# Summing the squares of the queries inside ACT's squaring instruction instead of in a DVE reduction (attention and mixture-of-experts kernel, one core)

## The chip, the cores and the metric

The kernel runs on one core of one Trainium2 chip. The metric is the device time of one execution in microseconds (us), less is better. The engines are called by the profile's names: PE is TensorE, DVE is VectorE, ACT is ScalarE, POOL is GpSimd, SP is the engine that here only issues transfers.

## The reference

One layer of a transformer, in float32: cross attention with normalised queries and keys, then a mixture of 12 experts, of which each token takes two.

```python
def rms_norm(x, w, eps=1e-6):
    var = mean(x * x, axis=-1)
    return w * (x * rsqrt(var + eps))

# x: (64, 128, 512), ctx: (64, 128, 512); 16 query heads, 4 key/value heads, 128 wide
q = (layernorm(x) @ Wq)   # (64, 128, 16 heads, 128)
k, v = ctx @ Wk, ctx @ Wv # (64, 128, 4 heads, 128)
q, k = rms_norm(q, q_norm_w), rms_norm(k, k_norm_w)
probs = softmax(q @ k.T / sqrt(128))          # each key head serves 4 query heads
x = x + (probs @ v) @ Wo
x = x + experts(layernorm(x))                 # top 2 of 12, with a capacity for each
```

The change touches the sum over the 128 columns of each query head in `rms_norm`.

## The kernel before, in words

**Two stages.** The first stage, some 2300 us of the 2700, does the attention and the routing of one batch of 128 tokens after the other, 64 batches, with batches 3 to 61 in a hardware loop (`loop`, L580). The second stage (`experts`, L33) gathers the tokens of each expert, computes and scatters them. The change is in the first stage alone.

**The unit of work.** A batch has four units, g = 0 to 3, one for each key head with its four query heads. Every engine has a function `body(b)` that runs through g = 0 to 3 and lists, by hand, what this engine does in this unit, in this order. An engine takes its instructions strictly in that order; between engines there are semaphores. The lists work at different distances from the current unit: the scores, exponentials and probabilities are those of the unit itself, the output projection that of two units back (`last`), the widened probabilities and the product with v one back (`before`), the scaled queries two ahead (`near`), and the projection and squares of the queries three ahead (`far`).

**Precision.** Each operand of a matmul is split in a high part (a cast on ACT) and a low part (a subtraction on DVE or POOL), and three products are summed.

**The queries, step by step.** PE projects four heads of queries to a PSUM bank (`queries`, L744). ACT squares the bank into another, SQ_B (`square_q`, L868 to L874). DVE sums the squares of each head (`sum_q`, L1013 to L1017). POOL adds the epsilon (L1289) and raises to the power -1/2 (`rms_q`, L1283 to L1292). One unit later ACT scales the queries by it, head by head, to f16 (`split_q`, L876 to L883), DVE forms the low part (L1019 to L1026), and SP issues a transposing transfer of both parts (`turn_q`, L622).

**The probabilities, step by step.** PE computes the scores (L752). DVE takes the maximum of each row (L1032) and its negative (L1035). ACT does the exponentials, head by head, each with its row sum from the accumulator (`exps`, L885 to L893). DVE inverts the sums (L1041) and multiplies (L1044). ACT casts the result to f16 (`split_p`, L899), DVE subtracts for the low part (L1050), SP issues the transposing transfer (`turn_p`, L627 to L630), and in the next unit ACT and DVE widen the transposed tile (L905, L1057). PE multiplies it with v (L764), ACT and DVE split the outcome (`split_o`, L911 and L971), and PE does the output projection (L780).

**The lists around the change.** On ACT a unit is: split_o, widen_p, one of (split_xn2, split_v, split_k) where g is 0, 1 or 3, exps, `square_q` of three units ahead, split_x (x_hi, L850, g = 0) or split_c (c_hi, L845, g = 3), split_p, split_q, and square_k where g = 1. On DVE it is: maxima, split_o, widen_p, some steps once a batch, normalise, `sum_q` of three units ahead, split_p, split_q, and again some steps once a batch. On POOL: split_x (x_lo, L1266, g = 0) or split_c (c_lo, L1261, g = 3), then rms_q, then small steps.

**Semaphores at the change.** Before squaring, ACT waits until the sum of the unit before is done (q_ss), and in the unit whose squares are those of g = 1 also until DVE has summed the squares of the keys, which use the same bank. DVE waits for the squares (q_sqd) and until POOL has read the sums before (q_m).

Of the kernel before, what the change touches and what calls it, by code (L numbers as in the profile page):

```python
# [11 lines left out]
HPG = NH // NG  # L12
# [16 lines left out]
QS, KS, PS = 16.0, 64.0, 16384.0  # L29
# [370 lines left out]
def build(nc, x, xT, cT, wq, wk, wv, wo, qw, kw, gateT, w13, w2T, out):  # L400
    f32, f32r, bf16, f16, i32, u32 = (mybir.dt.float32, mybir.dt.float32r, mybir.dt.bfloat16,
                                      mybir.dt.float16, mybir.dt.int32, mybir.dt.uint32)
    ACT = mybir.ActivationFunctionType
    AX = mybir.AxisListType
# [5 lines left out]
    def wait(eng, sem, n, apart=False):  # L410

        if isinstance(n, int) and n <= 0:
            return
        if apart:
            wait_apart(eng, (sem, n))
        else:
            eng.wait_ge(sem, n)

    def wait_apart(eng, *pairs):


        with ExitStack() as regs:
            values = []
            for s, n in pairs:
                if not isinstance(n, int):
                    reg = regs.enter_context(eng.register(f"wait_{s.name}_{nc.next_id()}"))
                    eng.reg_add(reg, n, 0)
                    n = reg
                values.append((s, n))
            eng.wait_ge(s_const, 1)  # L430
            for s, n in values:
                if not (isinstance(n, int) and n <= 0):
                    eng.wait_ge(s, n)  # L433

    def live(b):
        return not isinstance(b, int) or 0 <= b < NB

    def off(b, g, k):

        return b + (g + k) // NG, (g + k) % NG  # L440

    keep = ExitStack()
    with keep:
        def sem(name):
            return keep.enter_context(nc.semaphore(name))
# [11 lines left out]
        with ExitStack() as ctx:  # L457
# [35 lines left out]
            def sm(n, dt=f32):  # L493
                v = small[:, at[0]:at[0] + n]
                at[0] += n
                return v if dt is f32 else v.bitcast(dt)

            smax, nmax, psums, rsums = sm(4), sm(4), sm(4), sm(4)
            q_ssq, q_ms, q_rms = sm(4), sm(4), [sm(4), sm(4)]
# [15 lines left out]
            Q_BS, K_B, V_B, S_B, OT_B, WO_B, SQ_B = pb[0:2], pb[2], pb[3], pb[4], pb[5], pb[6], pb[7]  # L515

            def heads(bank):
                return bank[:, :].rearrange("p (h t) -> p h t", h=HPG)
# [14 lines left out]
            k_sqd, k_ss, k_m, k_r, k_nrm, k_hi, k_lo = (sem(n) for n in (  # L533
                "k_squared", "k_sumsq", "k_meansq", "k_rms", "k_normed", "k_hi", "k_lo"))
            v_hi, v_lo = sem("v_hi"), sem("v_lo")
            q_sqd, q_ss, q_m, q_r, q_hi, q_lo = (sem(n) for n in (
                "q_squared", "q_sumsq", "q_meansq", "q_rms", "q_hi", "q_lo"))
            sc_done, mx_done, nm_done, exp_done, rs_done, p_nrm, p_hi, p_lo = (sem(n) for n in (
                "scores_done", "max_done", "negmax_done", "exp_done", "rsum_done", "probs_done", "p_hi", "p_lo"))
            pt_hi, pt_lo, ot_done, ot_hi, ot_lo = (sem(n) for n in ("pt_hi", "pt_lo", "ot_done", "ot_hi", "ot_lo"))  # L540
# [18 lines left out]
            def stage(l):  # L559
                flat = work[:, STAGES[l % NST], :]  # L560
                return flat if LOTS[l][0] == "o" else flat.rearrange("p (c n) -> p c n", c=NC)
# [277 lines left out]
            def _(act):  # L839
# [28 lines left out]
                def square_q(b, g):  # L868
                    u = 4 * b + g
                    wait(act, q_done, u + 1)  # L870
                    wait(act, q_ss, u)
                    if g == 1:
                        wait(act, k_ss, b + 1)
                    nc.scalar.activation(SQ_B[:, :], Q_BS[g % 2][:, :], ACT.Square, scale=1.0 / QS).then_inc(q_sqd, 1)  # L874

                def split_q(b, g):  # L876
                    u = 4 * b + g
# [90 lines left out]
            def _(dve):  # L968
# [33 lines left out]
                def split_k(b):  # L1002
                    wait(dve, k_hi, b + 1)
                    nc.vector.tensor_tensor(s16[:, LO, :], kn.rearrange("p (g t) -> p g t", g=NG), s16[:, HI, :],
                                            ALU.subtract).then_inc(k_lo, 1)

                def split_v(b):
                    wait(dve, v_hi, b + 1)
                    nc.vector.scalar_tensor_tensor(out=vp[1][:, :, :], in0=V_B[:, :].rearrange("p (g t) -> p g t", g=NG),
                                                   scalar=1.0 / PS, in1=vp[0][:, :, :].bitcast(f32),  # L1010
                                                   op0=ALU.mult, op1=ALU.subtract).then_inc(v_lo, 1)

                def sum_q(b, g):  # L1013
                    u = 4 * b + g
                    wait(dve, q_sqd, u + 1)
                    wait(dve, q_m, u)
                    nc.vector.tensor_reduce(q_ssq, heads(SQ_B), AX.X, ALU.add).then_inc(q_ss, 1)  # L1017

                def split_q(b, g):  # L1019
                    u = 4 * b + g  # L1020
# [7 lines left out]
                def maxima(b, g):  # L1028
                    u = 4 * b + g
                    wait(dve, sc_done, u + 1)  # L1030
                    wait(dve, nm_done, u)
                    nc.vector.tensor_reduce(smax, heads(S_B), AX.X, ALU.max).then_inc(mx_done, 1)  # L1032
                    wait(dve, mx_done, u + 1)
                    wait(dve, exp_done, u)
                    nc.vector.tensor_scalar(nmax, smax, esc, -1.0, ALU.mult, ALU.mult).then_inc(nm_done, 1)  # L1035
# [17 lines left out]
                def widen_p(b, g):  # L1053
                    u = 4 * b + g
                    wait(dve, d_pT, 16 * (u + 1))
                    wait(dve, ot_done, u)
                    nc.vector.tensor_copy(ptp[1][:, :, :], pT16[:, LO, :]).then_inc(pt_lo, 1)  # L1057

                def split_o(b, g):
                    wait(dve, ot_hi, 4 * b + g + 1)  # L1060
                    minus([p[:, :, :] for p in otp], heads(OT_B)).then_inc(ot_lo, 1)

                def residual(b):
                    wait(dve, wo_used, 4 * b + 4)
                    wait(dve, d_xr, 16 * (b + 1))
                    nc.vector.tensor_tensor(x_res, x_res, WO_B[:, :], ALU.add).then_inc(x1_done, 1)
# [9 lines left out]
                def norm2(b):  # L1076
                    wait(dve, r2_done, b + 1)
                    wait(dve, d_x1, 16 * (b + 1))
                    nc.vector.tensor_scalar(x_res, x_res, mv_2[:, 0:1], rstd_2, ALU.subtract,
                                            ALU.mult).then_inc(xn2_done, 1)  # L1080

                def split_xn2(b):
                    wait(dve, xh_done, b + 1)
                    nc.vector.tensor_tensor(s16[:, LO, :], x_res.rearrange(by_chunk, c=NC), s16[:, HI, :],
                                            ALU.subtract).then_inc(xl_done, 1)
# [89 lines left out]
                for l in range(NLOT):  # L1175
                    if l + 1 < NLOT and LOTS[l + 1][0] == "q":
                        n, part = LOTS[l + 1][1], stage(l + 1)
# [12 lines left out]

                def body(b):
                    for g in range(NG):
                        cur, near, far = (b, g), off(b, g, 2), off(b, g, 3)
                        before, last = off(b, g, -1), off(b, g, -2)
                        if g == 2 and live(b - 1):
                            residual(b - 1)
                        if live(b):
                            maxima(*cur)
                        if live(last[0]):
                            split_o(*last)  # L1200
                        if live(before[0]):
                            widen_p(*before)
                        if g == 0 and live(b - 2):
                            split_xn2(b - 2)
                        if g == 1 and live(b):
                            split_v(b)
                        if g == 3 and live(b + 1):
                            split_k(b + 1)
                        if g == 3 and live(b - 1):
                            norm2(b - 1)  # L1210
                        if live(b):
                            normalise(*cur)
                        if g == 2 and live(b - 2):
                            copy_logits(b - 2)
                        if g == 3 and live(b - 2):
                            count(b - 2)
                        if live(far[0]):
                            sum_q(*far)
                        if live(b):
                            split_p(*cur)  # L1220
                        if live(near[0]):
                            split_q(*near)
                        if g == 0 and live(b + 1):
                            stats_x(b + 1)
                        if g == 0 and live(b - 3):
                            place(b - 3)
                        if g == 1 and live(b + 1):
                            sum_k(b + 1)
                        if g == 2 and live(b + 1):
                            norm_k(b + 1)  # L1230
                        if g == 2 and live(b - 2):
                            choose(b - 2)
                        if g == 2 and live(b - 1):
                            stats_2(b - 1)

                loop(dve, body)


# [133 lines left out]
```

## Time and profile before

| what | value |
|---|---|
| median of 3 runs | 2702.43 us (2699.23 to 2703.63) |
| the profiled execution's own time | 2700.49 us |
| span of its trace | 2698.8 us |
| PE busy in the span | 2445.5 us (91%) |
| DVE busy | 2081.5 us (77%) |
| ACT busy | 1646.8 us (61%) |
| POOL busy | 1106.9 us (41%) |

The span is the time from the first to the last instruction of one profiled execution; the rest of its time lies around it. The granted clock of PE is at full speed through the first stage, after its start. Durations of instructions on one engine overlap at their ends, so the time that an instruction takes from its queue is read from the start of one to the start of the next. The name `pb` is any of the eight PSUM banks, `work` the tiles of SBUF that hold probabilities, f16 parts and raw inputs, and `small` the columns of statistics.

### The profile page before, as it was taken

The page shows a single profiled execution, that of the slowest core. Times are in us where ns is not written, and L with a number is a line of the kernel's source. Part 1 is how long each engine was busy: PE and PEld are TensorE (multiplying, and loading weights), DVE is VectorE, ACT ScalarE, POOL GpSimd, SP SyncE. Part 2 cuts the span into 40 slices and gives each one's busy share as a digit, 9 for nine tenths or more (in the row PEclk, how much of TensorE's full clock was granted, in tenths as well). Part 3 has the DMA queues.
Part 4 walks back from the last instruction along what each step waited for, and adds up shares of the span by engine and source line. Part 5 has one row for each costly group of instructions (what it writes and reads, how often), then busy time and mean ns, then how long its engine had stood idle before and what let it go on. Part 6 is the DMA issues. An engine that isn't in the chain of part 4 may idle for free. (4 is left out here: it accounts for less than half of the span.)

```text
span 2698.8 us, 51748 instructions
## 1 busy us (share of the span) xinstructions
PE 2445.5 (91%) x12985; PEld 1883.8 (70%) x12985; DVE 2081.5 (77%) x5478; ACT 1646.8 (61%) x4789; POOL 1106.9 (41%) x1279
## 2 busy tenths in 40 slices
PE   3899999999999999999999999999999999739983
PEld 3677777777777777777777777777777777525541
DVE  5678888888888888888888888888888888626652
ACT  4566666666666666666666666666666666515541
POOL 0334334333333443433333334344333333248885
PEclk8999999999999999999999999999999999968775
DMA  7455555555555555555555555555555555439997
GB/s 210 85 114 115 120 122 117 117 123 118 123 117 118 113 116 124 117 118 119 121 121 119 119 112 115 123 120 118 117 124 117 124 113 111 89 107 182 183 176 96
DMA packets 778098, 331.20 MB, mean 123 GB/s; under 512 B 695340, under 2 KB 707884, under 8 KB 778032
## 3 DMA queue, kind: packets, MB, share of 16 engines
q1 hardware_dynamic: 754960, 287.61, 47.9%
q0 software_dynamic: 22912, 43.16, 8.9%
q8 instruction: 13, 0.21, 0.0%
q14 instruction: 21, 0.17, 0.0%
q10 hardware_dynamic: 192, 0.04, 0.0%
HBM read 108.15 MB, written 57.71 MB: 61 GB/s over the span
## 5 line engine op out<-in xcount | busy, mean ns | idle before, releaser
L905 ACT CAST pt_hi<-work 128x512 fp32r<-128x512 f16 x256 | 159.0, 621 | 652.6 <-DMA work<-work 652.6
L891 ACT ACTIVATE work<-pb,small 128x128 f32<-128x128 f32 x1024 | 454.0, 454 | 47.2 <-DVE small L1035 47.0
L788 PE MATMUL pb<-wo_hi,ot_hi 128*128 128x512 f32 x1024 | 418.8, 409 | 34.9 <-DVE ot_lo L971 34.8
L716 PE MATMUL pb<-wq_hi,x_hi 128*128 128x512 f32 x1024 | 400.9, 391 | 29.7 <-POOL x_lo L1266 22.5
L788 PE MATMUL pb<-wo_hi,ot_lo 128*128 128x512 f32 x1024 | 400.7, 391 | 0.0
L788 PE MATMUL pb<-wo_lo,ot_hi 128*128 128x512 f32 x1024 | 400.4, 391 | 0.0
L716 PE MATMUL pb<-wq_lo,x_hi 128*128 128x512 f32 x1024 | 400.0, 391 | 0.0
L716 PE MATMUL pb<-wq_hi,x_lo 128*128 128x512 f32 x1024 | 399.6, 390 | 0.0
L1289 POOL TENSOR_TENSOR small<-small 128x4 f32<-128x4 f32 x256 | 170.7, 667 | 500.3 <-DVE small L1017 500.3
L1023 DVE SCALAR_TENSOR_TENSOR work<-pb,small,work 128x128 f16<-128x128 f32 x1024 | 286.9, 341 | 47.1 <-ACT work L881 47.1
L881 ACT ACTIVATE work<-pb,small 128x128 f16<-128x128 f32 x1024 | 290.5, 365 | 0.5 <-DMA work<-work 0.4
L1292 POOL TENSOR_TENSOR small<-small 128x4 f32<-128x4 f32 x256 | 258.4, 1009 | 29.5 <-POOL small L1289 18.7
L1050 DVE TENSOR_TENSOR work<-work 128x512 f16<-128x512 f32 x256 | 250.2, 977 | 17.6 <-ACT work L899 11.6
L788 PEld LDWEIGHTS pb<-wo_hi,ot_hi 128*128 128x128 f32 x1024 | 192.6, 188 | 95.6 <-DVE ot_lo L971 61.7
L1266 POOL TENSOR_TENSOR x_lo<-work,x_hi 128x512 fp32r<-128x512 f32 x64 | 82.6, 1291 | 425.9 <-ACT x_hi L850 379.5
L716 PEld LDWEIGHTS pb<-wq_hi,x_hi 128*128 128x128 f32 x1024 | 192.7, 188 | 80.4 <-issue 28.5
L760 PEld LDWEIGHTS pb<-work 128*128 128x128 f16 x3072 | 172.8, 98 | 99.9 <-issue 57.1
L760 PE MATMUL pb<-work 128*128 128x128 f16 x3072 | 216.5, 220 | 22.7 <-DMA work<-work 21.3
L716 PE MATMUL pb<-wkv_hi,c_hi 128*128 128x512 f32 x512 | 223.0, 435 | 0.0
L788 PEld LDWEIGHTS pb<-wo_hi,ot_lo 128*128 128x128 f32 x1024 | 192.9, 188 | 42.4
L716 PEld LDWEIGHTS pb<-wq_hi,x_lo 128*128 128x128 f32 x1024 | 192.8, 188 | 40.9
L716 PEld LDWEIGHTS pb<-wq_lo,x_hi 128*128 128x128 f32 x1024 | 192.8, 188 | 39.1
(144 smaller groups left out, 5307.0 us busy)
## 6 DMA issues: line engine op xcount, KB each, us to landing
work<-x SPq DMA_DIRECT2D x128, 256.0 KB, 3.4
work<-cT SPq DMA_DIRECT2D x64, 256.0 KB, 2.7
work<-xT SPq DMA_DIRECT2D x64, 256.0 KB, 3.1
out<-work SPq DMA_DIRECT2D x64, 256.0 KB, 4.1
xn_scratch<-work SPq DMA_DIRECT2D x64, 256.0 KB, 2.2
work<-work SPq DMA_TRANSPOSE x640, 3.0
work<-wq SPq DMA_DIRECT2D x16, 256.0 KB, 3.4
work<-wo SPq DMA_DIRECT2D x16, 256.0 KB, 3.6
```

What stands on the lines that cost most here:

```text
L716: mm = nc.tensor.matmul(bank[:, :], lhs[a][:, c, :], rhs[b_][:, c, :], start=(c == 0 and n == 0), stop=(c == NC - 1 and n == 2))
L760: mm = nc.tensor.matmul(S_B[:, h * 128:(h + 1) * 128], qT16[:, 4 * a + h, :], kT16[:, 4 * b_ + g, :], start=(n == 0), stop=(n == 2))
L788: mm = nc.tensor.matmul(WO_B[:, :], otp[a][:, h, :], wop[b_][:, g * HPG + h, :], start=(g == 0 and h == 0 and n == 0), stop=(g == NG - 1 a ...
L881: hi = nc.scalar.activation(q16[:, h, :], Q_BS[g % 2][:, h * 128:(h + 1) * 128], ACT.Copy, scale=q_rms[g % 2][:, h:h + 1])
L891: ex = nc.scalar.activation(probs[:, cols], S_B[:, cols], ACT.Exp, bias=nmax[:, h:h + 1], scale=esc, accum_out=psums[:, h:h + 1])
L905: nc.scalar.copy(ptp[0][:, :, :], pT16[:, HI, :]).then_inc(pt_hi, 1)
L1023: lo = nc.vector.scalar_tensor_tensor(out=q16[:, 4 + h, :], in0=Q_BS[g % 2][:, h * 128:(h + 1) * 128], scalar=q_rms[g % 2][:, h:h + 1], in ...
L1050: nc.vector.tensor_tensor(p16[:, LO, :], probs.rearrange("p (h t) -> p h t", h=HPG), p16[:, HI, :], ALU.subtract).then_inc(p_lo, 1)
L1266: nc.gpsimd.tensor_tensor(xp[1][:, :, :], raw_x.rearrange(by_chunk, c=NC), xp[0][:, :, :].bitcast(f32), ALU.subtract).then_inc(x_lo, 1)
L1289: nc.gpsimd.tensor_tensor(q_ms, q_ssq, eps_x.broadcast_to([128, HPG]), ALU.add).then_inc(q_m, 1)
L1292: nc.gpsimd.tensor_tensor(q_rms[g % 2], q_ms, neghalf, ALU.pow).then_inc(q_r, 1)
```

## The change

ACT squares each of the four heads in an instruction of its own, of 128 columns, and has the sum of the results written to that head's column of `q_ssq` by the accumulator output. The fourth raises q_ss. The sum on DVE is gone, with the semaphore q_sqd; ACT now waits itself until POOL has read the sums of the unit before (q_m).

```diff
-            q_sqd, q_ss, q_m, q_r, q_hi, q_lo = (sem(n) for n in (
-                "q_squared", "q_sumsq", "q_meansq", "q_rms", "q_hi", "q_lo"))
+            q_ss, q_m, q_r, q_hi, q_lo = (sem(n) for n in (
+                "q_sumsq", "q_meansq", "q_rms", "q_hi", "q_lo"))
...
                 def square_q(b, g):
                     u = 4 * b + g
                     wait(act, q_done, u + 1)
-                    wait(act, q_ss, u)
+                    wait(act, q_m, u)
                     if g == 1:
                         wait(act, k_ss, b + 1)
-                    nc.scalar.activation(SQ_B[:, :], Q_BS[g % 2][:, :], ACT.Square, scale=1.0 / QS).then_inc(q_sqd, 1)
+                    for h in range(HPG):
+                        cols = slice(h * 128, (h + 1) * 128)
+                        sq = nc.scalar.activation(SQ_B[:, cols], Q_BS[g % 2][:, cols], ACT.Square, scale=1.0 / QS,
+                                                  accum_out=q_ssq[:, h:h + 1])
+                    sq.then_inc(q_ss, 1)
...
-                def sum_q(b, g):
-                    u = 4 * b + g
-                    wait(dve, q_sqd, u + 1)
-                    wait(dve, q_m, u)
-                    nc.vector.tensor_reduce(q_ssq, heads(SQ_B), AX.X, ALU.add).then_inc(q_ss, 1)
-
...
-                        if live(far[0]):
-                            sum_q(*far)
                         if live(b):
                             split_p(*cur)
```

## Rows read from the trace of the kernel before

**Rows 1.** The windows view, 300 to 2100 us: busy us and instructions of each engine, granted clock

```profile
300.00:2100.00 1800.00, 1734.11 (x9649) 1369.51 (x9648) 1493.60 (x4171) 1190.51 (x3605) 697.71 (x865) 1.00 0.54 118
```

**Rows 2.** The waits view, 300 to 2100 us: total us, times, longest us

```profile
ACT pt_hi L905 <- DMA work<-work: 513.7, 203, 3.1
ACT work L899 <- DVE work L1044: 49.3, 102, 0.5
...
ACT ot_hi L911 <- PE pb L776: 2.1, 12, 0.2
...
DVE small L1041 <- ACT work L891: 154.4, 152, 1.4
...
DVE work L1050 <- ACT work L899: 8.2, 51, 0.2
...
PE pb L806 <- DVE ot_lo L971: 26.4, 51, 0.9
PE pb L788 <- DVE ot_lo L971: 24.2, 51, 0.5
PE pb L760 <- DMA work<-work: 15.2, 50, 0.3
```

**Rows 3.** The time line of ACT, units 3 and 0: start us, duration us, instruction

```profile
1351.89 0.46 ACT L891 ACTIVATE work<-pb,small 128x128 f32<-128x128 f32 x1 [0.64 <-DVE small L1035]
1352.25 0.19 ACT L891 ACTIVATION_READ_ACCUMULATOR work<-pb,small 128x1 f32 x1
1352.34 0.45 ACT L891 ACTIVATE work<-pb,small 128x128 f32<-128x128 f32 x1
...
1353.65 0.60 ACT L874 ACTIVATE pb<-pb 128x512 f32<-128x512 f32 x1
1354.16 0.62 ACT L845 CAST c_hi<-work 128x512 fp32r<-128x512 f32 x1
1354.73 0.62 ACT L899 CAST work<-work 128x512 f16<-128x512 f32 x1
...
1359.84 0.62 ACT L905 CAST pt_hi<-work 128x512 fp32r<-128x512 f16 x1 [2.88 <-DMA work<-work]
...
1362.64 0.60 ACT L874 ACTIVATE pb<-pb 128x512 f32<-128x512 f32 x1
1363.15 0.62 ACT L850 CAST x_hi<-work 128x512 fp32r<-128x512 f32 x1
1363.80 0.62 ACT L899 CAST work<-work 128x512 f16<-128x512 f32 x1
```

**Rows 4.** The time line of DVE: L1050 in units 2, 3, 0, the sum in unit 3

```profile
1346.06 0.69 DVE L1050 TENSOR_TENSOR work<-work 128x512 f16<-128x512 f32 x1
...
1354.79 0.68 DVE L1017 TENSOR_REDUCE small<-pb 128x4 f32<-128x512 f32 x1
1355.39 1.30 DVE L1050 TENSOR_TENSOR work<-work 128x512 f16<-128x512 f32 x1
...
1364.45 1.23 DVE L1050 TENSOR_TENSOR work<-work 128x512 f16<-128x512 f32 x1 [0.16 <-ACT work L899]
```

**Rows 5.** Groups of instructions by line, ACT: count, busy us, mean ns, idle before them

```profile
L891 ACT ACTIVATE work<-pb,small 128x128 f32<-128x128 f32 x1024 | 454.0, 454 | 47.2 <-DVE small L1035 47.0
L881 ACT ACTIVATE work<-pb,small 128x128 f16<-128x128 f32 x1024 | 290.5, 365 | 0.5 <-DMA work<-work 0.4
L891 ACT ACTIVATION_READ_ACCUMULATOR work<-pb,small 128x1 f32 x1024 | 205.2, 200 | 0.0
```

**Rows 6.** The time line of ACT, unit 2: the square and the cast of the probabilities

```profile
1344.33 0.60 ACT L874 ACTIVATE pb<-pb 128x512 f32<-128x512 f32 x1
1345.41 0.62 ACT L899 CAST work<-work 128x512 f16<-128x512 f32 x1 [0.48 <-DVE work L1044]
```

**Rows 7.** The time line of POOL, units 3 and 0: the subtractions for c_lo and x_lo

```profile
1354.86 1.29 POOL L1261 TENSOR_TENSOR c_lo<-work,c_hi 128x512 fp32r<-128x512 f32 x1 [2.73 <-ACT c_hi L845]
...
1363.85 1.29 POOL L1266 TENSOR_TENSOR x_lo<-work,x_hi 128x512 fp32r<-128x512 f32 x1 [6.00 <-ACT x_hi L850]
```

More of the change, by code:

```diff
@@ L1192, in body @@
                     for g in range(NG):
-                        cur, near, far = (b, g), off(b, g, 2), off(b, g, 3)
+                        cur, near = (b, g), off(b, g, 2)
                         before, last = off(b, g, -1), off(b, g, -2)
```

## The prediction

> **What bounds the kernel now.** The window view of the middle 1800 us comes first [rows 1]. PE is busy 1734 us of them (96%), DVE 1494 us (83%), ACT 1191 us (66%), POOL 39%. By shares alone the edit looks good: it takes work from the fuller of the two vector engines and gives it to the emptier one. Shares are averages, so the waits of the same window come next [rows 2]. The reader is to see who waits for whom. PE waits only for DVE's ot_lo and for a transposed tile, 66 us in all. ACT and DVE almost never wait for PE: ACT has 2.1 us of it, DVE has none. So PE hangs on the others and they do not hang on it. Between themselves they form a ring: ACT waits 513.7 us, 203 times, for the transposed probabilities (pT), DVE waits 154.4 us for ACT's exponentials (L1041), ACT waits 49.3 us for DVE's normalised probabilities (L1044, before L899), and DVE waits 8.2 us for ACT's cast L899.
>
> The ring runs once per unit (one group of four heads, four units to a batch), by the program's order: pT lands; ACT widens it (L905) and, behind that in its queue, does the exponentials; DVE normalises; ACT casts (L899); DVE subtracts (L1050); SP issues the transpose; pT lands, about 3.15 us after the subtraction ends (1356.69 to 1359.84) [rows 3, 4]. Nothing in it is a matmul. A batch takes 1800/51 = 35.3 us (51 waits of the once-per-batch kind [rows 2]), so what is added to the ring per batch is added to the time some sixty times. The time lines show where in the ring the edit falls. I count units 0 to 3 by the g of the body.
>
> **The change, part by part.** *Removed: one DVE sum (L1017) per unit.* It starts at 1354.79 in unit 3 and the next DVE instruction, L1050, at 1355.39: 0.60 us of DVE's queue, 256 times, 154 us in all [rows 4]. It stands between the normalisation and the subtraction L1050. But L1050 needs ACT's cast L899, which in unit 3 runs 1354.73 + 0.62 = 1355.35 [rows 3], 0.04 us before L1050 starts. The sum fills time in which DVE would wait for that cast anyway. In unit 0 DVE even waits 0.16 us more after it. I take the gain as zero; its cover is the cast, and if the cast were not there it would be 0.60 us per unit. The semaphore between square and sum goes too; POOL's first step then follows ACT. POOL gets its sums earlier, but the scales are used a unit later and no ACT wait on them is in the list of waits, so this is zero too.
>
> *Added: ACT's one square of 512 columns becomes four of 128, each with a read of the accumulator.* The square occupies 1354.16 - 1353.65 = 0.51 us of the queue now [rows 3]. The trace has no square with a sum, so its price is bounded. The nearest row is the exponential L891: 454 ns, 128 columns, two operands from `small`, an accumulator read behind it [rows 5]. The read starts 0.36 us after the exponential and the next exponential 0.09 us after the read [rows 3]; one occupies (1353.65 - 1351.89)/4 = 0.44 us. The scaling copy L881 has one operand from `small` and lasts 365 ns, 89 less than the exponential. The square has none, so I take another 89 off: 276 ns. Less the overlap of 0.10 (0.454 against 0.36) and plus 0.09 for the read that is 0.27 us each, 1.08 for four. Lowest: the read hides wholly, 0.18 each, 0.72 for four. Upper for my own case: the second 89 ns is not saved, 0.36 each, 1.44. The highest end, a whole exponential, 0.44 each, 1.76, is a rival. I take 0.27, as the operand step is read from two rows. So ACT's queue gets 1.08 - 0.51 = **0.57 us longer per unit**.
>
> *Where it lies.* Units 1 and 2: ACT idles 0.48 us before L899, waiting for L1044 [rows 2, 6]. From the start of the square to the start of L899 are 1345.41 - 1344.33 = 1.08 us. The four squares just fit: zero, and 4p - 1.08 if one takes p and p is above 0.27.
>
> Unit 3: after the square comes the cast of the next context, c_hi (L845, starts 1354.16), then L899 at 1354.73. There is 0.05 us of slack at most. c_hi starts 0.57 later. POOL's subtraction c_lo (L1261) starts at 1354.86, within 0.1 us of c_hi's end, and runs 1.29 us to 1356.15 [rows 7]. It matters, because L1050 lasts 1.30 us here, against 0.69 in unit 2, and ends at 1356.69, 0.54 us after POOL: it seems to stand still until POOL is through [rows 4, 6, 7]. So its end moves with c_hi: +0.57. Behind it the transpose is issued 0.57 later, pT lands 0.57 later, and unit 0's L905 and exponentials start 0.57 later.
>
> Unit 0 repeats this: square at 1362.64, x_hi (L850) at 1363.15 [rows 3], POOL's x_lo (L1266) 1363.85 to 1365.14 [rows 7], L1050 ending at 1364.45 + 1.23 = 1365.68, again 0.54 us after POOL. Another +0.57.
>
> One rule of the pages bears on this. The Trainium skill, "SBUF — State Buffer", section "Who interferes with whom", says that a DVE instruction with two SBUF inputs and a GpSimd instruction that reads SBUF exclude each other, and that the one that starts first holds the other off for its whole length. By that rule the trace agrees (end of L1050 = end of POOL + 0.54, twice). Had L1050 only been slower in itself, the shift would go through L899 alone, which has 0.09 us of slack in unit 3 (0.05 in ACT's queue, 0.04 in DVE's) and 0.13 in unit 0 (it starts at 1363.80, and could at 1363.67): some 0.92 us per batch and 56 us in all instead of 70.
>
> *Order and queues.* The new wait of the square (POOL's first step of the unit before) is met a unit earlier, as POOL works in order and is idle most of a unit: zero. The wait that keeps the key squares from the shared bank is now met by ACT's own earlier instruction. Behind the longer square stand, in ACT's queue, c_hi or x_hi, L899, the scaling copies and ot_hi. Those last feed PE through DVE's ot_lo, and PE will wait longer there, as a result and not as a cause. SP's queue is only moved with L1050; no transfer is added or changes place.
>
> **The sum.** 0.57 + 0.57 + 0 + 0 = 1.14 us per batch. c_hi is cast in unit 3 of 62 batches, x_hi in unit 0 of 63; the first one or two run behind the loading of weights. I take 61: 61 x 1.14 = **70 us**. The profiled execution took 2700.49 us (span 2698.8, 1.7 around it), which gives 2770; the median of the runs shown is 1.9 us higher, 2702.43, so 2772. Bounds of my case: at 0.18 each, 0.21 x 2 = 0.42 per batch, 26 us, 2728; at 0.36 each, (0.93 + 0.36) x 2 = 2.58 per batch, 157 us, 2860.
>
> **The rivals.** *Faster, by DVE's queue.* Place: L1050 in unit 3, where DVE has no idle time at all and L1050 starts the instant the sum ends. If DVE's own order sets that moment, 0.60 us fall away in that unit: 61 x 0.60 = 37 us, 2666. For it: 83% busy, and L1041 does not wait there (152 waits for 203 units [rows 2]). Against it: the cast ends 0.04 us before, and POOL's pass holds L1050 beyond that. It would decide only if the four squares took no more of ACT than the one (0.13 us each) and POOL did not hold L1050. The Trainium skill, "Perfetto Trace Analysis", section "Optimizing Scalar/DVE Operations", says that if DVE is saturated, moving work to Scalar may make sense; no row shows DVE saturated where this work lies, since it waits in three units of four.
>
> *No change.* ACT waits 513.7/51 = 10.1 us per batch for pT, and PE is 96% busy. If either were true slack, 1.14 us would vanish in it: 2702. Against it: the landing of pT is itself released by L1050, so it moves with ACT; and PE waits for DVE.
>
> *A whole exponential's price.* At 0.44 each: 1.76 - 0.51 = 1.25 twice, and 1.76 - 1.08 = 0.68 twice, 3.86 per batch, 235 us, 2938. For it: it is the one measured form with a sum. Against: the operand step of 89 ns.
>
> That the change does not do what it says I set aside; the sums and the order are plain in the diff.
>
> **How the numbers follow.** My case 0.80, faster 0.06, no change 0.07, the full exponential 0.07. The three rivals are the 0.20 that may be left out, so the range is my case's own, 2728 to 2860. A measurement of this kernel can tell about 0.2% from no change. Slower: 0.80 + 0.07 = 0.87; same 0.07; faster 0.06.
>
> **What would show it.** Right: square rows of about 276 ns with reads of 0.20; the ACT queue from the first square to c_hi about 1.08 us; L1050 in units 3 and 0 still ending 0.54 us after POOL, and now waiting for L899 in all units; ACT's idle time before L899 near zero; PE's waits for ot_lo up by about 1 us per batch with PE's busy share down to 93%; a batch of 36.4 us. Wrong: a batch still at 35.3 us, ACT's wait for pT shorter by what the squares cost, or L1050 in unit 3 earlier against L1041 than now.

## The result and the profile after

The change made the kernel slower: 2791.7 us (median of 4 runs, 2789.7 to 2793.0) against 2701.3 us, ratio 1.033 (95% interval 1.032 to 1.035), 90 us more. The forecast was 2772 us with a range from 2728 to 2860.

The windows view of the kernel after, 300 to 2100 us, with the same columns as [rows 1]:

```profile
300.00:2100.00 1800.00, 1678.12 (x9261) 1312.47 (x9260) 1327.05 (x3794) 1238.91 (x4822) 612.21 (x829) 1.00 0.52 114
```

PE is busy 93% of the time and not 96%, at the same granted clock. DVE went from 83% to 74%, ACT only from 66% to 69%. DVE got its relief, and it bought nothing. The waits of the same window are to be read beside [rows 2]; the line numbers have shifted, so that ACT's widening cast is L909, the cast of the probabilities L903, and DVE's subtraction L1048:

```profile
ACT pt_hi L909 <- DMA work<-work: 524.0, 195, 3.3
...
DVE work L1048 <- ACT work L903: 179.7, 195, 1.3
DVE small L1039 <- ACT work L895: 158.3, 147, 1.6
...
PE pb L716 <- DVE work L1021: 44.2, 49, 0.9
PE pb L806 <- DVE ot_lo L975: 37.3, 48, 1.2
PE pb L788 <- DVE ot_lo L975: 25.0, 49, 0.5
PE pb L760 <- DMA work<-work: 15.3, 50, 0.3
```

The reader is to see two things. DVE's wait for ACT's cast rose from 8.2 us to 179.7 us, about 0.92 us per unit: the time of the removed sum (0.60 us) and, in units 3 and 0, that of the longer squares stand there as idle time. And ACT no longer waits for DVE's L1044 at all (49.3 us before): its idle time before the cast is used up. The groups of ACT instructions, as in [rows 5], have the new work:

```profile
L876 ACT ACTIVATE pb<-pb 128x128 f32<-128x128 f32 x1024 | 283.2, 277 | 18.4 <-PE pb L716 18.4
...
L876 ACT ACTIVATION_READ_ACCUMULATOR pb<-pb 128x1 f32 x1024 | 201.8, 197 | 0.0
```

Next the time line of ACT in unit 3, as in [rows 3] (of the four squares the first two stand here), and the instructions of POOL and DVE behind it, as in [rows 7] and [rows 4]:

```profile
1369.57 0.28 ACT L876 ACTIVATE pb<-pb 128x128 f32<-128x128 f32 x1
1369.76 0.20 ACT L876 ACTIVATION_READ_ACCUMULATOR pb<-pb 128x1 f32 x1
1369.85 0.28 ACT L876 ACTIVATE pb<-pb 128x128 f32<-128x128 f32 x1
...
1370.70 0.62 ACT L845 CAST c_hi<-work 128x512 fp32r<-128x512 f32 x1
1371.21 0.63 ACT L903 CAST work<-work 128x512 f16<-128x512 f32 x1
...
1376.38 0.62 ACT L909 CAST pt_hi<-work 128x512 fp32r<-128x512 f16 x1 [2.94 <-DMA work<-work]
```

```profile
1371.39 1.28 POOL L1257 TENSOR_TENSOR c_lo<-work,c_hi 128x512 fp32r<-128x512 f32 x1 [3.35 <-ACT c_hi L845]
```

```profile
1371.87 1.35 DVE L1048 TENSOR_TENSOR work<-work 128x512 f16<-128x512 f32 x1 [1.08 <-ACT work L903]
```

The squares take 1370.70 - 1369.57 = 1.13 us of ACT's queue, where the one square took 0.51. POOL's pass ends at 1372.67 and L1048 at 1373.22, again 0.55 us later, though DVE had stood idle 1.08 us before it.

**Where the 90 us are.** The table is worked out from the traces: for each unit between 300 and 2100 us, the time from the start of the widening cast pt_hi to the start of the next one (one turn of the ring), split at the end of DVE's subtraction (L1050 of before); means over about 50 batches, in us.

| unit | before: to the end of the subtraction + to pT | after | more |
|---|---|---|---|
| 0 | 5.84 + 3.27 = 9.11 | 6.45 + 3.28 = 9.73 | 0.62 |
| 1 | 5.19 + 3.30 = 8.49 | 5.23 + 3.51 = 8.74 | 0.25 |
| 2 | 4.73 + 3.27 = 8.00 | 4.75 + 3.28 = 8.03 | 0.03 |
| 3 | 6.70 + 3.15 = 9.85 | 7.29 + 3.15 = 10.44 | 0.60 |
| batch | 35.45 | 36.94 | 1.49 |

61 x 1.49 = 91 us, the whole of the result. (From the first pt_hi to the last, the trace after is 93.2 us longer than the one before, and all that lies behind the last is 1.9 us shorter.) Units 0 and 3 are as argued. In unit 1, 0.21 of the 0.25 us lie behind the subtraction, in the transposing transfer. Nothing of that was forecast.

### The profile page after: what moved, and what is told of

It is laid out like the page before. It is cut to its first block and busy times, and to the rows that moved or that the text cites. A ratio compares the mean times of both kernels' runs of the same rounds, so it can differ in the third digit from the quotient of the medians.

```text
span 2790.4 us, 53029 instructions
## 1 busy us (share of the span) xinstructions
PE 2462.0 (88%) x12985; PEld 1877.6 (67%) x12985; DVE 1943.4 (70%) x5222; ACT 1773.9 (64%) x6581; POOL 1029.9 (37%) x1279
## 5 line engine op out<-in xcount | busy, mean ns | idle before, releaser
L909 ACT CAST pt_hi<-work 128x512 fp32r<-128x512 f16 x256 | 159.0, 621 | 686.9 <-DMA work<-work 686.9
L716 PE MATMUL pb<-wq_hi,x_hi 128*128 128x512 f32 x1024 | 409.3, 400 | 85.0 <-DVE work L1021 63.0
L1048 DVE TENSOR_TENSOR work<-work 128x512 f16<-128x512 f32 x256 | 259.9, 1015 | 237.5 <-ACT work L903 237.5
L716 PE MATMUL pb<-wq_hi,x_lo 128*128 128x512 f32 x1024 | 400.8, 391 | 0.0
L716 PE MATMUL pb<-wq_lo,x_hi 128*128 128x512 f32 x1024 | 400.8, 391 | 0.0
L1021 DVE SCALAR_TENSOR_TENSOR work<-pb,small,work 128x128 f16<-128x128 f32 x1024 | 286.8, 341 | 53.6 <-ACT work L885 53.6
L1285 POOL TENSOR_TENSOR small<-small 128x4 f32<-128x4 f32 x256 | 107.3, 419 | 524.8 <-ACT pb L876 524.8
L716 PEld LDWEIGHTS pb<-wq_hi,x_hi 128*128 128x128 f32 x1024 | 193.4, 189 | 155.5 <-DVE work L1021 84.0
L876 ACT ACTIVATE pb<-pb 128x128 f32<-128x128 f32 x1024 | 283.2, 277 | 18.4 <-PE pb L716 18.4
L1288 POOL TENSOR_TENSOR small<-small 128x4 f32<-128x4 f32 x256 | 258.0, 1008 | 29.5 <-POOL small L1285 18.7
L716 PE MATMUL pb<-wkv_hi,c_hi 128*128 128x512 f32 x512 | 223.3, 436 | 0.1
L716 PEld LDWEIGHTS pb<-wq_hi,x_lo 128*128 128x128 f32 x1024 | 193.4, 189 | 41.7
```

Source lines behind the costliest of these rows:

```text
L716: mm = nc.tensor.matmul(bank[:, :], lhs[a][:, c, :], rhs[b_][:, c, :], start=(c == 0 and n == 0), stop=(c == NC - 1 and n == 2))
L876: sq = nc.scalar.activation(SQ_B[:, cols], Q_BS[g % 2][:, cols], ACT.Square, scale=1.0 / QS, accum_out=q_ssq[:, h:h + 1])
L909: nc.scalar.copy(ptp[0][:, :, :], pT16[:, HI, :]).then_inc(pt_hi, 1)
L1021: lo = nc.vector.scalar_tensor_tensor(out=q16[:, 4 + h, :], in0=Q_BS[g % 2][:, h * 128:(h + 1) * 128], scalar=q_rms[g % 2][:, h:h + 1], in ...
L1048: nc.vector.tensor_tensor(p16[:, LO, :], probs.rearrange("p (h t) -> p h t", h=HPG), p16[:, HI, :], ALU.subtract).then_inc(p_lo, 1)
L1285: nc.gpsimd.tensor_tensor(q_ms, q_ssq, eps_x.broadcast_to([128, HPG]), ALU.add).then_inc(q_m, 1)
```

## The experiments

Each run was compared with the kernel before on the same chip; its median there was between 2690 and 2700 us, so ratios are what is compared, not times. Where an edit speaks of "the kernel after", it starts from the changed kernel.

### The removed sum by itself: sum_gone

On the kernel after, ACT squares all 512 columns in one instruction again, and no engine sums; the norms of the queries are left out.

```diff
+                nc.vector.memset(q_ssq, 1.0)
...
-                    for h in range(HPG):
...
-                    sq.then_inc(q_ss, 1)
+                    nc.scalar.activation(SQ_B[:, :], Q_BS[g % 2][:, :], ACT.Square, scale=1.0 / QS).then_inc(q_ss, 1)
```

> The kernel after, with ACT's square again one instruction of 512 columns and no sum of the squares on any engine (the sums are left at a constant, so the norms of the queries are left out). It shows the removal of DVE's sum alone. My theory, that ACT's cast covers the sum: 2701 us as before, or up to 13 us more if POOL's scatter, which now comes earlier, lengthens the transpose of unit 1. Rival, that DVE's own queue set L1050 in unit 3: 61 x 0.60 = 37 us less, 2664.

Measured: ratio 1.019 (1.017 to 1.021), 52 us slower than before. The scatter had been allowed at most 13 us. Less work on DVE, the square on ACT as it was, and slower. Three units are as before (9.13, 7.99, 9.83 us), and so is unit 1 up to the end of the subtraction (5.19); but there the transpose took 4.18 us from issue to landing, where it takes 3.23 in before and 3.44 in the kernel after. SP's and POOL's time lines show what changed: the issue of the transpose, and the start of the scatter. First of before, then of the kernel after, then of this run:

```profile
1374.28 1.24 SPq L630 DMA_TRANSPOSE work<-work  x1
```

```profile
1375.61 1.11 POOL L1304 DMA_INDIRECT token_table<-small  x1 [0.18 <-issue]
```

```profile
1354.52 1.24 SPq L630 DMA_TRANSPOSE work<-work  x1
```

```profile
1354.85 1.11 POOL L1300 DMA_INDIRECT token_table<-small  x1 [0.19 <-issue]
```

```profile
1371.52 1.25 SPq L630 DMA_TRANSPOSE work<-work  x1
```

```profile
1371.48 1.11 POOL L1297 DMA_INDIRECT token_table<-small  x1 [0.19 <-issue]
```

Once a batch, in unit 1, POOL scatters routing entries, behind rms_q in its queue. rms_q waits for the sum of the squares. In before the scatter starts 1.33 us after the issue of the transpose; in the kernel after the sums come from ACT earlier and it starts 0.33 us after; here 0.04 us ahead. This offset hardly varies over the trace (for the kernel after from 0.32 to 0.33 us).

### The same without the collision: sum_gone_scatter_late and scatter_late

```diff
+                        if g == 1 and live(b + 1):
+                            rms_k(b + 1)
                         if g == 1 and live(b - 3):
                             scatter(b - 3)
-                        if g == 1 and live(b + 1):
-                            rms_k(b + 1)
```

> The kernel without any sum of the squares, in which the scatter started 0.04 us before the issue of the transpose and that transpose took 4.18 us, with the scatters moved behind rms_k in the same way. Theory of the collision: the transpose takes 3.2 us again, a batch 35.4 us, the time that of before (ratio 1.000, within 0.3%). That would leave nothing for the removed sum itself. If the sum had been worth 0.60 us in unit 3, it would show now: ratio 0.986. If the scatter is not the cause: ratio 1.019 as before.

Measured: 0.9986 (0.9976 to 0.9996). The scatter starts 3.63 us after the issue, the transpose takes 3.23 us, a batch 35.43 us. So the sum on DVE, removed at no cost elsewhere, is worth 0.14%, and no more than 0.24% by the interval: it was covered, as forecast. The same move of the scatters on the kernel after:

> The kernel after, with POOL's two scatters moved behind rms_k in unit 1, so that they start some 4 us after the transpose of the probabilities is issued and not 0.3 us. Theory of the collision: issue to landing in unit 1 goes from 3.44 back to 3.2 us, 0.21 x 61 = 13 us less than the kernel after (ratio 1.033 of before becomes 1.028). If the longer transpose came from something else, the loads say: no change, 1.033.

Measured: 1.029 (1.028 to 1.031); unit 1 went from 8.74 to 8.53 us, the transpose from 3.44 to 3.23. The collision is thus 0.21 x 61 = 13 us of the 90 by the traces (by the two ratios 10 us, give or take 6), and the rest, some 77 us, is the length of the squares.

### What the length of the squares costs: four_squares and both_sums

```diff
-                    nc.scalar.activation(SQ_B[:, :], Q_BS[g % 2][:, :], ACT.Square, scale=1.0 / QS).then_inc(q_sqd, 1)
+                    for h in range(HPG):
+                        cols = slice(h * 128, (h + 1) * 128)
+                        sq = nc.scalar.activation(SQ_B[:, cols], Q_BS[g % 2][:, cols], ACT.Square, scale=1.0 / QS)
+                    sq.then_inc(q_sqd, 1)
```

> The kernel before, with the square cut in four of 128 columns without accumulator, and DVE's sum kept. In the kernel after one square with its read took 0.28 us of the queue, of which the read about 0.09; so 0.19 each, 0.76 for four, 0.25 more than the one. In units 3 and 0 that is 0.50 per batch, 61 x 0.50 = 30 us: 2731. If only the accumulator reads cost anything: 2701.

Measured: 1.009 (1.007 to 1.011), 24 us; a batch 0.34 us longer, nearly all of it in units 3 and 0. The time line of ACT in unit 3:

```profile
1367.77 0.78 ACT L876 ACTIVATE pb<-pb 128x128 f32<-128x128 f32 x4
1368.43 0.65 ACT L845 CAST c_hi<-work 128x512 fp32r<-128x512 f32 x1
```

The four take 0.66 us, 0.165 each and not 0.19. Cutting the square costs 0.15 us a unit, and the accumulator reads the rest of the 0.62: 1.13 - 0.66 = 0.47, or 0.12 each. I had put a read at 0.09.

both_sums is this edit with the accumulator output and the wait for q_m added, and DVE's sum kept.

> The accumulating squares on ACT and DVE's sum as well. My theory: DVE's sum is hidden behind the later cast, and the ring is longer by ACT alone. As POOL starts again only after DVE's sum, its scatter should not move against the transpose in unit 1: 2779 us, with 3.2 us from issue to landing there. If the scatter has nothing to do with it: 2792. If DVE's sum had been a saving in the kernel after: 2792 + 37 = 2829.

Measured: 1.032 (1.030 to 1.033), 2776 us against 2691 on that chip. Unit 0 took 9.75 us, unit 3 10.35, as in the kernel after (9.73, 10.44). The transpose of unit 1 took 3.22 us with POOL again behind DVE's sum (offset 1.34 us), which is the collision theory's mark. But units 1 and 2 (8.62 and 8.12 us) were each 0.09 us longer than with the scatter late: DVE's sum can start only when the longer squares are through, and so it ends after ACT's cast, which no longer covers all of it. In unit 3, 0.06 us of this come back. The collision that is missing and the sum that is no longer hidden nearly cancel, and the time alone, which I had set as the test, would not have told them apart; the transfer's time does.

### Place and not load: hybrid

In the bodies g = 1 and 2 (queries of g = 0 and 1) accumulating squares, in the others the square and the sum of before:

```diff
+                    if g >= 2:
+                        nc.scalar.activation(SQ_B[:, :], Q_BS[g % 2][:, :], ACT.Square,
+                                             scale=1.0 / QS).then_inc(q_sqd, 1)
+                        return
+                    wait(act, q_m, u)
+                    for h in range(HPG):
...
-                        if live(far[0]):
+                        if live(far[0]) and far[1] >= 2:
                             sum_q(*far)
```

> The accumulating squares only in the bodies g = 1 and g = 2, where ACT idled 0.48 us; in g = 3 and g = 0 the square and DVE's sum stay as before. My theory: 0.06 us per batch, 4 us, and 13 more if the earlier scatter of unit 1 lengthens the transpose: 2705 to 2718. Rival, that it is ACT's load as such and not the place: half of what the change cost, 2746.

Measured: 1.008 (1.006 to 1.010), 22 us, a quarter of the change for half of its instructions. This is just above the forecast (ratio 1.006 at most). Of 0.37 us per batch 0.21 are the collision (3.43 us in unit 1, offset 0.33), 0.06 the squares, and 0.08 are in unit 3. These last stand in front of the exponentials and not at the squares. DVE's maximum starts 0.2 us after the instruction ahead of it and not 0.1, as the same two rows show, first of before, then of this run, and ACT waits for it:

```profile
1350.80 0.18 DVE L1074 BATCH_NORM_AGGREGATE small<-small 128x2 f32<-128x6 f32 x1
1350.90 0.69 DVE L1032 TENSOR_REDUCE small<-pb 128x4 f32<-128x512 f32 x1
```

```profile
1364.55 0.18 DVE L1083 BATCH_NORM_AGGREGATE small<-small 128x2 f32<-128x6 f32 x1
1364.76 0.69 DVE L1041 TENSOR_REDUCE small<-pb 128x4 f32<-128x512 f32 x1
```

```profile
1365.75 0.46 ACT L900 ACTIVATE work<-pb,small 128x128 f32<-128x128 f32 x1 [0.82 <-DVE small L1044]
```

What DVE does in the extra 0.1 us is not shown. The same 0.62 us of ACT cost about 0.6 in units 0 and 3 of the kernel after and 0.02 to 0.04 in units 1 and 2, in both kernels.

### What holds DVE's subtraction: the casts first

```diff
-                        if live(far[0]):
-                            square_q(*far)
                         if g == 0 and live(b + 1):
                             split_x(b + 1)
                         if g == 3 and live(b + 2):
                             split_c(b + 2)
+                        if live(far[0]):
+                            square_q(*far)
```

On the kernel after:

> The kernel after, with the same two casts ahead of the four squares. By my theory the casts, and POOL behind them, are early again, L899 is late by the squares, and L1050 then starts after POOL is through and takes 0.69 us: it ends 1.64 + 0.62 + 0.03 + 0.69 = 2.98 us after the exponentials, against 3.04 in the kernel before. So units 3 and 0 cost what they cost before, and what is left is 0.06 of the squares and 0.21 of the collision in units 1 and 2: some 10 us over before, ratio 1.004, against 1.033 of the change. If L1050 were slow in itself (1.3 us in these units whatever POOL does): 1.2 us per batch more, ratio 1.031.

Measured: 1.0065 (1.004 to 1.009) against 1.033: one change of order gives back most of the loss. Unit 0 is 9.05 us and unit 3 9.79, both 0.06 below before, as worked out. DVE in unit 3 and in unit 0, and POOL's passes beside it:

```profile
1364.14 0.69 DVE L1048 TENSOR_TENSOR work<-work 128x512 f16<-128x512 f32 x1
1373.06 0.69 DVE L1048 TENSOR_TENSOR work<-work 128x512 f16<-128x512 f32 x1 [1.25 <-ACT work L903]
```

```profile
1362.55 1.50 POOL L1257 TENSOR_TENSOR c_lo<-work,c_hi 128x512 fp32r<-128x512 f32 x1 [2.23 <-ACT c_hi L845]
1371.46 1.50 POOL L1262 TENSOR_TENSOR x_lo<-work,x_hi 128x512 fp32r<-128x512 f32 x1 [5.76 <-ACT x_hi L850]
```

The subtraction takes 0.69 us in these units too, once POOL is through before it starts (at 1364.05 and 1372.96). Its 1.3 us were a wait. Unit 1 took 8.87 us, 0.13 more than in the kernel after, of which I had not thought. The traces show where: with unit 0 shorter, DVE comes late to the maximum of unit 1. L1033 starts 0.89 us after pt_hi instead of 0.46, and the exponentials 1.16 us after it instead of 1.01 (means of 50 batches). So part of what unit 0 gains meets DVE's own queue one unit later.

On the kernel before:

> The kernel before, with c_hi and x_hi cast ahead of the square on ACT in units 3 and 0. My theory, that POOL's subtraction behind these casts holds L1050: POOL's pass starts 0.51 us earlier in both units, L1050 ends 1.98 + 0.54 = 2.52 us after the exponentials leave ACT's queue and not 3.04; 1.04 us per batch, 63 us less (ratio 0.977), if PE, which then waits for less than 1 us per batch, doesn't take over; with that 0.977 to 0.985. If L1050 is just slow in these units or follows the cast L899 alone: no change, ratio 1.000.

Measured: 1.0023 (1.001 to 1.003). A miss: not 63 us less but 6 more. Unit 0 gained 0.29 us and not 0.52, unit 3 lost 0.37. DVE in unit 3, and POOL in units 3 and 0:

```profile
1356.65 0.69 DVE L1044 SCALAR_TENSOR_TENSOR work<-work,small 128x512 f32<-128x512 f32 x1
1357.26 0.17 DVE L1113 TENSOR_TENSOR small<-pb,small 128x24 f32<-128x24 f32 x1
1357.35 1.17 DVE L1115 TENSOR_TENSOR macc<-macc,small 128x24 bf16<-128x24 bf16 x1
1358.44 0.68 DVE L1017 TENSOR_REDUCE small<-pb 128x4 f32<-128x512 f32 x1
1359.04 0.68 DVE L1050 TENSOR_TENSOR work<-work 128x512 f16<-128x512 f32 x1
```

```profile
1356.98 1.50 POOL L1261 TENSOR_TENSOR c_lo<-work,c_hi 128x512 fp32r<-128x512 f32 x1 [2.22 <-ACT c_hi L845]
...
1366.37 1.50 POOL L1266 TENSOR_TENSOR x_lo<-work,x_hi 128x512 fp32r<-128x512 f32 x1 [5.50 <-ACT x_hi L850]
```

POOL's pass, begun while L1044 ran, takes 1.50 and not 1.29 us, in both units; in unit 0 that is what is missing of the gain. And in unit 3 a tiny instruction, L1115, 160 ns in the mean before, stands 1.17 us, until POOL ends at 1358.48. L1113 just ahead of it, with one input from PSUM, runs through in 0.17. The sum L1017 and L1050 stand behind L1115. Here, for once, DVE's sum is on the ring.

### Untangling it: x_first, c_before_exps, count_behind

x_first moves split_x alone, and leaves unit 3 as in before.

> The kernel before, with x_hi alone cast ahead of the square, in unit 0; unit 3 as before. In the run with both casts first, unit 0 fell from 9.11 to 8.82 us and unit 3 rose from 9.85 to 10.22, because POOL's earlier pass there held DVE's update of the expert counts (L1115), with the sum L1017 behind it. My theory: unit 0 keeps its 0.29 us and unit 3 is 9.85 again: 61 x 0.29 = 18 us less, ratio 0.993. If the two units are not independent: 1.000.

Measured: 0.9930 (0.991 to 0.995), 19 us less; unit 0 8.84 us, unit 3 9.81.

c_before_exps adds to it:

```diff
+                        if g == 3 and live(b + 2):
+                            split_c(b + 2)
                         if live(b):
                             exps(*cur)
```

> The kernel before, with x_hi ahead of the square in unit 0 and c_hi ahead of the exponentials in unit 3, where ACT idles 0.64 us for DVE. POOL's pass for c_lo then runs beside DVE's L1004 and not beside L1050. My theory: L1004 is held 0.3 us, L1050 takes 0.69 instead of 1.30 us and ends 0.28 us earlier; with the 0.29 of unit 0 0.57 per batch, 35 us less, ratio 0.987. If PE takes over, which waited 1.3 us per batch: between that and 0.993.

Measured: 0.9982 (0.997 to 0.999), a miss, and worse than x_first: unit 0 as there, unit 3 10.03 us. L1050 did take 0.69 us. But POOL, early now, caught another instruction of DVE, the cast L1057:

```profile
1350.87 1.29 DVE L1057 CAST pt_lo<-work 128x512 fp32r<-128x512 f16 x1
```

```profile
1350.59 1.29 POOL L1261 TENSOR_TENSOR c_lo<-work,c_hi 128x512 fp32r<-128x512 f32 x1
```

The cast takes 0.42 us elsewhere and 1.29 here, and this delay of 0.87 us is on DVE's path to L1044. I had only reckoned with instructions that read SBUF twice. The Trainium skill, "SBUF — State Buffer", section "Who interferes with whom", lists casts among the instructions that can enter a mode in which DVE takes the ports that it shares with GpSimd. By that the trace agrees (0.42 us against 1.29), and read against every DVE instruction in reach of POOL's pass it could have warned of the miss.

after_best is this order on the kernel after, with the scatters late.

> The kernel after with the same order of the casts and the scatters behind rms_k. Unit 3: the normalised probabilities are there 1.35 us after the exponentials leave ACT's queue, the four squares take 1.13 of it, so they are hidden, and L1050 ends 0.3 us earlier than in before. Unit 0: as in the run of the kernel after with the casts first, 0.06 less than before. Units 1 and 2: 0.07 more. Sum -0.3 per batch, 18 us less than before, ratio 0.993; so with this order too, the kernel with DVE's sum is the faster of the two. If the accumulating form were better once nothing waits for it: below 0.987.

Measured: 1.0063 (1.005 to 1.008), also a miss by the same mechanism (the same cast held for 1.29 us; unit 3 9.99 us). The comparison with c_before_exps holds: with the same casts in the same places the accumulating form is 0.8% behind the form with DVE's sum, though its scatters are out of the way.

count_behind has both casts first and takes the held instruction out of the way:

```diff
-                        if g == 3 and live(b - 2):
-                            count(b - 2)
                         if live(far[0]):
                             sum_q(*far)
                         if live(b):
                             split_p(*cur)
+                        if g == 3 and live(b - 2):
+                            count(b - 2)
```

> The kernel before, with both casts ahead of the square, and with DVE's update of the expert counts (L1113, L1115) moved behind the subtraction L1050 in unit 3. With the casts alone moved, POOL's pass for c_lo began between DVE's L1044 and L1115, held L1115 for 1 us, and the sum and L1050 stood behind it. My theory: with the counts out of the way L1050 is what POOL holds, it ends about 2.74 us after the exponentials leave ACT's queue as in unit 0, and not 3.04; unit 3 is 9.55 us, unit 0 8.82, together 0.59 per batch, 36 us less than before, ratio 0.987. If the cause of the slower unit 3 was another: ratio 1.002 as with the casts alone.

Measured: 0.9876 (0.986 to 0.989), 2665 us against 2700 on its chip, 35 us less: the fastest version of this study, with DVE's sum in it. DVE and POOL in unit 3:

```profile
1371.49 0.69 DVE L1017 TENSOR_REDUCE small<-pb 128x4 f32<-128x512 f32 x1
1372.09 0.99 DVE L1050 TENSOR_TENSOR work<-work 128x512 f16<-128x512 f32 x1
```

```profile
1371.04 1.50 POOL L1261 TENSOR_TENSOR c_lo<-work,c_hi 128x512 fp32r<-128x512 f32 x1 [2.22 <-ACT c_hi L845]
```

L1050 is held again, until 0.54 us after POOL's end (1372.54 and 1373.08), but earlier than in before. The split is not quite as foretold: unit 3 is 9.69 us, not 9.55, and unit 2 is 0.12 shorter by its transfer; the total of 0.55 per batch agrees with the 0.59 expected. The two belong together. In unit 3 the exponentials wait for DVE's maximum and not for the transfer, here as in before ([rows 3], the 0.64 us), so a tile that lands 0.13 us earlier only waits: the exponentials start 2.03 us after pt_hi, where they start 1.87 after it with the casts alone moved. PE now waits 50.5 us in the window for the moved counts. That costs nothing that can be seen, as unit 0 (8.84 us) and unit 1 (8.50 us) are as long as without it; but PE has hardly another wait left and is 97% busy, so little more can be won in the ring.

## Why the prediction was right, point by point

**The bound.** PE hangs on a ring of ACT, DVE, POOL and one transfer. Right: a batch took 35.45 us before and 36.94 after, the difference stands unit by unit in the ring, and PE merely waited more. One arc of it was misread: in unit 3 the exponentials hang on DVE's queue and its maximum (L1035), and not on the landing of pT, as the row with 0.64 us in [rows 3] already shows. It cost the forecast nothing, since nothing in unit 2 was moved, but count_behind and after_casts_first met it.

**The removed sum is covered.** Right, by sum_gone_scatter_late: 0.14%, at most 0.24%, where DVE's own queue would have given 1.4%. This also settles the rival that forecast a faster kernel. The cover holds in this order only: in before_casts_first the sum stood on the ring.

**The semaphore and POOL's order: zero.** This step failed. I saw that POOL gets its sums earlier and asked only who uses the scales. The question left out was what stands behind rms_q in POOL's queue: the scatter, which came 1 us earlier and met the transpose of unit 1. It cost 13 us here, and 52 us in sum_gone, where it came 0.37 us earlier still. The prediction also said that SP's queue only moves with L1050, which was true; the two transfers meet from different queues.

**The price of the squares.** The estimate of 276 ns for one was right (277). Its place in the queue was 0.28 us and not 0.27, because the read takes 0.12 and not 0.09 of it (four_squares). Four are 1.13 us, 0.62 more than the one; 0.57 was forecast. In units 0 and 3 that is 0.05 each, 6 us of the sum. In units 1 and 2, 1.13 no longer fits in the 1.08 us there: measured 0.04 + 0.02, some 3 us.

**The sum.** 70 forecast; 70 + 6 + 3 + 13 = 92, against 90 measured. That the scatter fell inside the range is luck: the range was made from the price of a square alone. The rivals "no change" and "a whole exponential's price" (0.44 each) fell with the measured 0.28.

**Who holds L1050.** Right, and the larger part of what there was to learn. L1050 ended 0.54 to 0.55 us after POOL in before, in the kernel after and in count_behind, and took 0.69 us where POOL was through. But I weighed this wait on one instruction only. POOL's pass also held L1115, with two SBUF inputs, and the cast L1057, with one, and three of my expectations failed there (before_casts_first, c_before_exps, after_best).

**What the profile was to show.** A batch of 36.4 us came as 36.9, PE's share 93% and DVE's wait for the cast in all units (195 times) as said. PE's longer wait did not fall on ot_lo as I wrote (62 us in the window, 51 before): most of it is a new wait of the query projection for q_lo (44 us, PE L716 <- DVE L1021).

## What to carry to other kernels

Before work is moved from a full engine to an emptier one, look in the time line for what releases the instruction behind it: work that sits in a wait is free on the full engine, and on the emptier one its place in the queue sets its price (0.62 us of ACT cost about 0.6 in two units and 0.02 to 0.04 in the other two). When a semaphore fires earlier, follow every instruction behind the waiting one, its transfers too; an earlier start can cost time. And if a pass on GpSimd lies beside the critical engine, check all DVE instructions in its reach, and not the one that you want to free.

## What the runs showed of the hardware that was not expected

A scatter of POOL (two indirect transfers, 1.1 and 1.0 us on the engine) lengthens a transposing transfer of SP by how close it starts to the transpose's issue: 1.33 us after it or later, nothing (3.22 to 3.24 us from issue to landing); 0.33 us after it, 0.21 us more; 0.04 us ahead of it, 0.95 us more. Four kernels with the offset 0.33 or 0.04 and ten with 1.33 or more agree. Which resource the two share was not tried.

POOL's subtraction holds DVE's instructions with two SBUF inputs and a cast with one, and is itself 0.21 us longer when it starts within such an instruction. A 24-column addition on DVE took 1.17 us for that reason. Instructions with an input from PSUM were not held beside it: in before_casts_first L1113 took 0.17 us, and the sum L1017 of unit 0, begun 0.52 us into POOL's pass, 0.69 us.
